# Wide attention of a 16-head layer: the value product with the values stationary, softmax sums by a block of ones, and a new order of the pieces

## The reference, cut to what matters

```
b, s, _ = x.shape
q = (x @ Wq).reshape(b, s, N_HEADS, HEAD_DIM)
k = (x @ Wk).reshape(b, s, N_HEADS, HEAD_DIM)
v = (x @ Wv).reshape(b, s, N_HEADS, HEAD_DIM)
dot = jnp.einsum('bihd,bkhd->bhik', q, k)
w = jax.nn.softmax(dot / jnp.sqrt(jnp.float32(HEAD_DIM)), axis=-1)
a = jnp.einsum('bhij,bjhd->bihd', w, v)
a = a.reshape(b, s, N_HEADS * HEAD_DIM)
return a @ Wo + bo
```

## Time and profile before

| | us |
|---|---|
| median of 3 runs | 2512.74 |
| lowest and highest | 2504.58, 2514.27 |
| the profiled execution | 2513.31 |
| its span, first to last instruction | 2511.3 |
| first matmul of the wide block, to the last DVE instruction of it | 56.9 to 787.3 |

### The profile page before, as it was taken

The page is one execution under the profiler, slowest core; times in us unless marked ns, Lnnn a source line. Parts: engine busy times, 40 slices in busy tenths (PEclk is TensorE's granted clock), DMA queues, the critical chain, the costliest instruction groups (busy, mean ns, idle before and its releaser), DMA issues. The chain is left out here.

```text
span 2511.3 us, 53791 instructions
## 1 busy us (share of the span) xinstructions
PE 2157.5 (86%) x21439; PEld 1560.5 (62%) x21439; DVE 1429.7 (57%) x2854; ACT 1158.7 (46%) x1979; POOL 602.0 (24%) x952
## 2 busy tenths in 40 slices
PE   0899999999998799788868998999669997469996
PEld 0687877877787689655547896666435543234543
DVE  1545454454542443466644445776568885768883
ACT  0333333333324233366553323665647775537774
POOL 4111111111100322133203232443123331433330
PEclk9999999999997899899978998999869998669998
DMA  5000000000000002245400022444134440034441
GB/s 156 1 1 1 1 1 1 1 1 1 1 1 1 6 5 51 51 108 117 95 2 4 1 52 53 109 116 93 25 84 107 110 105 2 2 92 108 107 106 49
DMA packets 142790, 121.04 MB, mean 48 GB/s; under 512 B 11808, under 2 KB 127408, under 8 KB 142548
## 3 DMA queue, kind: packets, MB, share of 16 engines
q1 hardware_dynamic: 142548, 117.64, 19.7%
HBM read 63.48 MB, written 54.12 MB: 47 GB/s over the span
## 5 line engine op out<-in xcount | busy, mean ns | idle before, releaser
L890 DVE TENSOR_REDUCE l_group_mx<-maxima 128x4 f32<-128x1024 f32 x248 | 303.9, 1226 | 77.1 <-PE maxima L683 75.6
L2059 ACT ACTIVATE l_wide_pr<-scores 128x512 f32<-128x512 f32 x256 | 139.0, 594 | 408.7 <-PE scores L2003 408.7
L818 ACT ACTIVATE l_group_pr<-scores 128x1024 f32<-128x1024 f32 x256 | 261.7, 1022 | 72.2 <-PE scores L704 70.0
L2014 PEld LDWEIGHTS bank<-l_wide_va,l_wide_pr 128*128 128x128 f32 x2048 | 254.2, 192 | 36.0 <-issue 33.2
L2014 PE MATMUL bank<-l_wide_va,l_wide_pr 128*128 128x65 f32 x2048 | 254.5, 271 | 0.0
L2098 DVE TENSOR_REDUCE l_wide_mx<-maxima 128x2 f32<-128x512 f32 x256 | 165.1, 687 | 92.2 <-PE maxima L1983 92.2
L2157 POOL CAST l_wide_qk<-l_wide_qk 128x512 bf16<-128x512 f32 x128 | 78.7, 615 | 390.6 <-ACT l_wide_qk L2054 390.6
L890 DVE TENSOR_REDUCE l_slope_mx<-maxima 128x6 f32<-128x768 f32 x124 | 118.9, 959 | 78.2 <-PE maxima L690 76.8
L890 DVE TENSOR_REDUCE l_rope_mx<-maxima 128x6 f32<-128x768 f32 x124 | 118.8, 958 | 58.8 <-PE maxima L690 57.9
L818 ACT ACTIVATE l_slope_pr<-scores 128x768 f32<-128x768 f32 x128 | 103.6, 810 | 91.0 <-PE scores L711 90.8
L724 PE MATMUL bank<-l_group_pr,va 128*32 128x256 f32 x2048 | 145.3, 403 | 0.0
(11 more groups left out here) (456 smaller groups left out, 4721.5 us busy)
## 6 DMA issues: line engine op xcount, KB each, us to landing
l_group_st<-stack_dram SPq DMA_DIRECT2D x64, 384.0 KB, 6.0
l_slope_st<-stack_dram SPq DMA_DIRECT2D x32, 384.0 KB, 5.6
l_rope_st<-stack_dram SPq DMA_DIRECT2D x32, 384.0 KB, 5.6
stack_dram<-l_group_parts SPq DMA_DIRECT2D x64, 192.0 KB, 2.3
stack_dram<-l_group_parts SPq DMA_DIRECT2D x64, 128.0 KB, 1.9
stack_dram<-l_slope_parts SPq DMA_DIRECT2D x32, 192.0 KB, 2.4
stack_dram<-l_rope_parts SPq DMA_DIRECT2D x32, 192.0 KB, 2.3
stack_dram<-l_slope_parts SPq DMA_DIRECT2D x32, 128.0 KB, 2.3
```

Of the source, the lines that this page charges most:

```text
L818: act.activation(pr[:, i % AHEAD, :, 0:keys], Tp[:, :, 0:keys], ACT.Exp).then_inc(s["exps"], 1)
L890: dve.tensor_reduce(mx[:, b % 2, :, :, i], max_bank(i, b)[:, :, 0:BLOCKS * keys].rearrange("p z (a k) -> p z a k", k=keys), AX.X, ALU.max, ...
L2014: ins = pe.matmul(Ob[i // 2 % 2][:, col:col + D64 + 1], pr[:, i % WIDE_AHEAD, kt * S + t * P:kt * S + (t + 1) * P], va[:, par, kt, i, :], ...
L2059: act.activation(pr[:, h % WIDE_AHEAD, :], Tb[h % 2][:], ACT.Exp).then_inc(s["exps"], 1)
```

## The change

The value product is turned round. For a pair of heads the values are stationary, 128 keys by 64 channels, and 256 columns of `pr` (all queries) move; the first head's output lies on PSUM partitions 0 to 63 and the second's on 64 to 127, which puts the two into the left and the right half of PE's columns. The output has channels on partitions, as "project" needs it, so "attn", `att` and the copies to `att_t` are gone. The softmax sums come from a piece of their own, "sum": POOL adds the two key tiles of `pr` into `tiles_sum`, and PE multiplies them by a 128 x 64 block of ones, so the sum stands on the same 64 partitions as the head's values. DVE then takes the reciprocal of all 128 x 256 of them and multiplies. ACT copies the values "v" in place of DVE. "project" is cut into two halves of 128 rows.

The order is new: `wide_slots` has eight slots, one for each pair i, and each holds divide i-2, score i, max i+1, qk i+2, value and sum i-1, and at most one or two of v, xn, norm, project, turnmax, split. `wide_walk` writes out the steps and gives the banks `Mb` in turn. In batch 0 the maxima of odd pairs use the banks `Tb`.

```diff
-WIDE_BANK = {"norm": (0,), "qk": (1, 0, 1, 0, 1, 0, 1, 0), "attn": (1, 0, 1, 0), "v": (1, 0, 1, 0), "project": (1,),
-             "turnmax": (0,)}
-WIDE_AHEAD = 4
...
+def wide_slots():
+    slots = []
+    for i in range(PAIRS):
+        slot = [("divide", (i - 2) % PAIRS, -1 if i < 2 else 0), ("score", i, 0)]
+        slot += [("turnmax", 0, 1)] if i == 7 else []
+        slot += [("max", (i + 1) % PAIRS, 2 if i + 1 >= PAIRS else 1)]
+        slot += [("split", 0, 1)] if i == 6 else []
+        slot += [("qk", (i + 2) % PAIRS, 2 if i + 2 >= PAIRS else 1)]
+        slot += [(what, (i - 1) % PAIRS, -1 if i < 1 else 0) for what in ("value", "sum")]
+        slot += {1: [("v", 0, 1)], 2: [("v", 1, 1)], 3: [("v", 2, 1), ("xn", 0, 2)], 4: [("project", 0, -1)],
+                 5: [("v", 3, 1), ("norm", 0, 2)], 6: [("project", 1, -1)]}.get(i, [])
+        slots += slot
+    return slots
+
+
+def wide_walk():
+
+    slots, order, counts = wide_slots(), [], [0, 0]
+    bank = {}
+    for what, i, _ in slots:
+        if what in ("norm", "qk", "v", "project", "turnmax"):
+            bank[what, i] = len(bank) % 2
+    for n in range(-2, NB + 1):
+        for what, i, ahead in slots:
+            if 0 <= n + ahead < NB:
+                m = bank.get((what, i))
+                if m is not None:
+                    counts[m] += 1
+                order.append((what, i, n + ahead, m, counts[m] if m is not None else None))
+    return order
...
-        va = sb("va", [P, 2, NT, H, D64 + 1])
+        va = sb("va", [P, 2, NT, H, D64])
+        ones = sb("ones", [P, D64])
...
-        pr = sb("pr", [P, WIDE_AHEAD, 2 * S])
-        rc = sb("rc", [P, 4])
-        att = sb("att", [P, 2, NT, H, D64])
-        att_t = sb("att_t", [P, PAIRS, S])
+        pr = sb("pr", [P, 2, 2, 2 * S])
+        tiles_sum = sb("tiles_sum", [P, 2, 2, S])
+        rc = sb("rc", [P, S])
+        att_t = sb("att_t", [P, 2, PAIRS, S])
...
+        def max_banks(i, b):
+            return Tb if b == 0 and i % 2 else Sb
...
-                    elif what == "value":
-                        if i % 2 == 0:
-                            wait(pe, s["divided"], o_t.add() - 2)
-                        pe.wait_ge(s["exps"], exps_t.add())
-                        for t in range(NT):
-                            col = ((i % 2) * NT + t) * (D64 + 1)
-                            for kt in range(NT):
-                                ins = pe.matmul(Ob[i // 2 % 2][:, col:col + D64 + 1],
-                                                pr[:, i % WIDE_AHEAD, kt * S + t * P:kt * S + (t + 1) * P], va[:, par, kt, i, :],
-                                                start=(kt == 0), stop=(kt == NT - 1))
-                        ins.then_inc(s["valued"], 1)
...
-                    elif what == "attn":
-                        if i == 0:
-                            pe.wait_ge(s["divided"], divided_t.add(PAIRS))
-                        for c in range(2):
-                            for t in range(NT):
-                                ins = pe.transpose(bank[:, (c * NT + t) * P:(c * NT + t + 1) * P],
-                                                   att[:, nxt, t, 4 * i + 2 * c:4 * i + 2 * c + 2, :].rearrange("p h d -> p (h d)"),
-                                                   K.ident[:])
-                        ins.then_inc(full[b], 1)
...
+                elif what == "max":
+                    pe.wait_ge(s["half"], p + 1)
+                    wait(pe, s["maxed"], 2 * p - (0 if b else 2))
...
+                elif what == "score":
+                    if i == 0:
+                        copied(pe, "turnmax", 0, b)
+                    wait(pe, s["exps"], 2 * p)
...
+                elif what == "value":
+                    if i == 0:
+                        copied(pe, "v", 3, b)
+                    wait(pe, s["divided"], p - 1)
+                    pe.wait_ge(s["exps"], 2 * p + 2)
+                    for kt in range(NT):
+                        for z in range(2):
+                            ins = pe.matmul(Ob[i % 2][rows(z), 0:S], va[:, at, kt, 2 * i + z, :],
+                                            pr[:, i % 2, z, kt * S:(kt + 1) * S], start=(kt == 0), stop=(kt == NT - 1))
+                    ins.then_inc(s["valued"], 1)
+                elif what == "sum":
+                    pe.wait_ge(s["added"], 2 * p + 2)
+                    for z in range(2):
+                        ins = pe.matmul(Ob[i % 2][rows(z), S:2 * S], ones[:], tiles_sum[:, i % 2, z, :], start=True, stop=True)
+                    ins.then_inc(s["summed"], 1)
+                elif what == "project":
+                    pe.wait_ge(s["divided"], PAIRS * (b + 1))
+                    for c in range(PAIRS):
+                        ins = pe.matmul(bank[:, 0:C], att_t[:, at, c, i * P:(i + 1) * P], W["wo"][:, c, :],
+                                        start=(c == 0), stop=(c == PAIRS - 1))
+                    ins.then_inc(full[m], 1)
...
+                elif what == "v":
+                    act.wait_ge(full[m], count)
+                    act.activation(va[:, at, i // 2, 8 * (i % 2):8 * (i % 2) + 8, :].rearrange("p h d -> p (h d)"),
+                                   Mb[m][:], ACT.Copy).then_inc(drained[m], 1)
+                elif what == "score":
+                    wait(act, s["valued"], p - 1)
+                    wait(act, s["added"], 2 * (p - 1))
+                    for z in range(2):
+                        act.wait_ge(s["scored"], 2 * p + z + 1)
+                        act.activation(pr[:, i % 2, z, :], Tb[z][:], ACT.Exp).then_inc(s["exps"], 1)
...
-                    elif what == "divide":
-                        dve.wait_ge(s["valued"], valued_t.add(2))
-                        o = Ob[i % 2][:, 0:2 * NT * (D64 + 1)].rearrange("p (z t e) -> p t z e", z=2, t=NT)
-                        r = rc[:].rearrange("p (t z) -> p t z", t=NT)
-                        wait(dve, s["divided"], divided_t.value())
-                        own.done(dve.reciprocal(r, o[:, :, :, D64]))
-                        divided_t.add()
-                        dve.tensor_tensor(att[:, par, :, 2 * i:2 * i + 2, :], o[:, :, :, 0:D64],
-                                          r.unsqueeze(3).to_broadcast([P, NT, 2, D64]), ALU.mult).then_inc(s["divided"], 1)
...
+                elif what == "divide":
+                    dve.wait_ge(s["summed"], p + 1)
+                    wait(dve, s["divided"], p)
+                    own.done(dve.reciprocal(rc[:], Ob[i % 2][:, S:2 * S]))
+                    dve.tensor_tensor(att_t[:, at, i, :], Ob[i % 2][:, 0:S], rc[:], ALU.mult).then_inc(s["divided"], 1)
+                elif what == "project":
+                    tile = b * NT + i
+                    dve.wait_ge(s["biased"], b + 1)
+                    dve.wait_ge(full[m], count)
+                    dve.tensor_tensor(K.X[:, tile, :], K.X[:, tile, :], Mb[m][:, 0:C], ALU.add).then_inc(drained[m], 1)
+                    dve.wait_ge(drained[m], count)
+                    dve.bn_stats(K.moments[:, tile, :], K.X[:, tile, :]).then_inc(s["stats"], 1)
...
+                elif what == "score":
+                    wait(pool, s["summed"], p - 1)
+                    for z in range(2):
+                        pool.wait_ge(s["exps"], 2 * p + z + 1)
+                        pool.tensor_tensor(tiles_sum[:, i % 2, z, :], pr[:, i % 2, z, 0:S], pr[:, i % 2, z, S:2 * S],
+                                           ALU.add).then_inc(s["added"], 1)
```

More of the change, by code:

```diff
@@ L1905, in wide_attention @@
 def wide_attention(nc, K, name, W):
-    fills = [sum(b == m for banks in WIDE_BANK.values() for b in banks) for m in range(2)]
     with ExitStack() as ctx:
@@ L1933, in wide_attention @@
         block = ctx.enter_context(nc.Block(name))
-        POOL_SETS = 6
-        def rows(h):
-            return slice(64 * (h % 2), 64 * (h % 2) + 64)
-        def fill_tallies():
-            return [Tally(s["full0"], fills[0]), Tally(s["full1"], fills[1])]
-        def bank_of(tallies, what, i):
-            if what not in WIDE_BANK:
-                return None, None
-            b = WIDE_BANK[what][i]
-            return b, tallies[b].add()
+        POOL_SETS = 7
+        order = wide_walk()
@@ L1948, in _, with rows, copied @@
+        filling = {(what, i, b): (m, count) for what, i, b, m, count in order}
+        def rows(z):
+            return slice(64 * z, 64 * z + 64)
+        def max_banks(i, b):
+            return Tb if b == 0 and i % 2 else Sb
+        def copied(eng, what, i, b):
+            m, count = filling[what, i, b]
+            eng.wait_ge(drained[m], count)
         @block.tensor
         def _(pe):
-            fill = fill_tallies()
-            xn_t, half_t, maxed_t = Tally(s["xn"], 1), Tally(s["half"], PAIRS), Tally(s["maxed"], H)
```

265 lines of the change are left out of this document (88 added, 177 removed).

## The result

| | before | after |
|---|---|---|
| median, us | 2509.22 (4 runs) | 2437.23 (4 runs) |
| lowest and highest | 2504.58, 2514.27 | 2431.62, 2445.55 |
| span of the profiled execution | 2511.3 | 2443.4 |
| last DVE instruction of the wide block ends | 787.3 | 719.6 |
| from there to the end of the span | 1724.0 | 1723.8 |

The ratio is 0.9715, with a 95% interval of 0.9679 to 0.9752: 72 us faster. 2426 was forecast, with 2404 to 2470 as its range, that is a gain of 87 us. The last two rows say where the time came from: the wide block is 67.7 us shorter and the layers behind it take what they took. Between kernels whose later layers are the same instructions that rest varied in the profiles from 1713 to 1726 us, so for edits of the wide block its end is the sharper measure than the time of the launch.

What follows compares the result with a forecast made beforehand. PE was taken as the bound; start 88.0, low clock 3.1, batches 35.0, 504.4, 36.1 and 24.6, tail 9.2 end the wide block at 700.4, not 787.3. 2513.3 less 86.9 gives 2426 us, range 2404 to 2470.

Steps and rivals of the forecast that it cites:

- The bound: Wide block: PE's pieces add up to the batch before and after; DVE, ACT and POOL stay below it.
- Value and sum: PE, per pair: 6 rounds of 0.215 plus 0.14, 1.43 us, in place of 1.86 for two heads' values.
- the quarters of the group layer: Pricing row: value with four heads in quarters of the columns, 16 records in 1.00 us, running four at a time.
- The rival that halves overlap in part: PE's value and sum gain only 1.6 times, 1.75 us a pair, 41 us more: 2467 us; chance 0.10.
- the one that they don't: PE's value and sum in halves never overlap, 2.72 us a pair, 165 us more: 2591 us; chance 0.05.
- The slot and the batch: PE: ordinary slot 3.80 us; eight of them plus v, project, norm and turnmax make 38.8, against 44.53 before.
- DVE: Reciprocal of 128 x 256 at 1.75 us, batch work 29.2; rival with DVE as bound: 2466 us, chance 0.15.
- The margin in slots 7 and 0: About 0.3 us between the end of DVE's maxima and PE's max, after the split and the wait for project.
- ACT and POOL: Work per batch 16.9 and 17.3 us, neither bounding; POOL's adds must not delay the cast for PE's next max.
- The first score: Start of block on PE: at 88 us, each pair waiting 3.0 for qk, copy, cast and max; half-clock rival: 2433.
- The low clock that follows the first score: Wide block after 88.0 us: 3.1 us added, as 7.50 us at clock 0.59 before, assumed to happen again.
- The tail: End of wide block: sum 7 waits for adds, then two divides of 2.25 and both projects in a row, 9.2 us.

Runs made afterwards that it cites:

- Experiment 3: Kernel after, with the reciprocal of only 128 of the 256 columns of sums, used for both halves: 2437.6 us, ratio 0.9724 to the kernel before.
- experiment 6: Kernel after without POOL's adds, PE's sum multiplying both key tiles, four products in place of two: 2497.5 us, ratio 0.9946 to the kernel before.
- experiment 5: Kernel after with each head's value product on all 128 columns, outputs of the two heads mixed: 2551.9 us, ratio 1.018 to the kernel before.
- experiment 1: Kernel after with v, norm, xn and project moved between qk and value of their slot: 2419.7 us, ratio 0.9653 to the kernel before.
- experiment 4: Kernel after with each reciprocal done twice: 2505.7 us, ratio 0.9985 to the kernel before.
- experiment 2: Kernel after with qk i+2 ahead of max i+1 in the steps before the first scores: 2432.9 us, ratio 0.972 to the kernel before.
- experiment 8: Kernel after with v, norm, xn, project between qk and value, and qk ahead of max before the first scores: 2415.2 us, ratio 0.963 to the kernel before.

## Why the prediction was right, and what it mis-sized

*The bound.* PE alone, before and after: right. Experiment 3 shows it for DVE, where half of the new work changed no batch, and experiment 6 for POOL, where taking the adds away gave nothing back.

*Value and sum.* 1.43 us a pair was forecast from the quarters of the group layer, 1.44 was measured. The rival that halves overlap in part is out (0.91 against 1.82 in experiment 5), so is the one that they don't: two halves gained 2.0. Had they not overlapped the kernel would have been slower, by 1.8% for the values alone (2551.9); the rival's 2591 counts the sums too.

*The slot and the batch.* 3.80 was forecast and 3.91 measured, 38.8 and 40.0. This is the step that was too small. I had priced qk, v and project from rows in which a piece on the full array followed them. The 0.11 of "handover" that I added to a qk's 0.86 is the price of coming back to the full array from a max; the 0.09 of leaving it was missing. In the new order it falls on the eight qk, which stand ahead of a value in halves, 0.7 us a batch, on three of the four v, 0.3 (the fourth stands ahead of norm and costs the old 0.97), and on the halves of project, 0.2. Experiment 5 shows it the other way: with the value on the full array, qk costs 0.97 again. The Trainium skill, "TensorEngine Tiling (Array Packing)", section "Key Properties", says that changing the tiling mode drains the TensorE. The trace agrees in that a change costs time (0.2 us for a v's stretch, experiment 1); of a drain itself it shows only that the next weight load doesn't start ahead. I had left the rule out of the sum because the number of changes a pair seemed to fall.

*DVE.* The reciprocal was forecast at 1.75 us from three rows of 4 to 32 columns; it is 1.753. (The sum as written, 353 + 224 x 6.2, gives 1.742.) The Trainium skill's repeat count of 8 ("VectorE: DVE Perf Modes", the 8-slice pipeline), from which 2.3 us were estimated, doesn't fit if it is read as eight cycles a column: 954 ns for 128 columns and 1753 for 256 are 6.24 ns a column. DVE's busy time a batch was forecast at 29.2 and is 30.2; the reciprocals are not the cause, 8 x 1.753 being the 14.0 of the sum, and where the 1.0 lies was not traced. The margin in slots 7 and 0 was forecast at 0.3 us and is 1.0 (the maxima end at 405.70, PE's max starts at 406.72), in part since I counted gaps where the records overlap (experiment 4).

*ACT and POOL.* 16.9 and 17.3 a batch forecast, 16.8 and 16.5 measured; the adds are hidden (experiment 6).

*The ends.* The first score was forecast at 88 and came at 89.8. I had the chain at full clock, 3.0 us a pair, and one us for a slow start; it ran at 4.08 for three pairs, 3.86 for one and 2.92 from there. The low clock that follows the first score in the earlier trace rows didn't come back (fast records and 1.00 from 90 us on), 3.1 less. That was luck: experiments 3 and 4 have the same instructions up to the first score, and their clock fell there, to 0.68 and 0.63 from 88 to 91 us, though it cost them less than 3.1, some 1.3 us in experiment 3. The tail was forecast at 9.2 and took 11.1, 1.6 of it by the low clock in project. The errors sum up: 1.8 for the start, 15.0 for the batches (18 less the 3.1), 0.5 and 1.9 for the last batch and the tail, 19.2 in all, which is 719.6 against 700.4. The launch came out only 11 us above the forecast, because the profiled execution was the slowest of the four, 8 us above their median, while the forecast was summed from a profiled execution close to its median: that too is luck, and the gain that was forecast, 87 us, was 15 too large.

## What to carry to other kernels

On PE, count the stretches on the full array in the written order as well as the columns: pieces that use the whole array belong side by side, and putting them so was worth 17 us here with the same instructions. When a piece is priced from a row, look at what stands ahead of it and behind it there, and whether both will be of the same shape in the new place. Turning a product round so that its narrow side fills half of the array paid here only since two such products run beside each other (without it the kernel is 1.8% slower) and since the sums are made cheap elsewhere: POOL's hidden adds were 55 of the 72 us, and without them the turned product was no better than the old one in the same order. Price an instruction of a new size from a line through several sizes of the same operation; it gave the reciprocal within 1%.

## What the runs showed of the hardware that was not expected

- A reciprocal on DVE costs 6.24 ns a column (954 ns at 128, 1753 at 256), so 256 columns take four times what a multiply of that shape takes (424 ns). An operation that was negligible at four columns became DVE's largest.
- A qk of four records costs 0.86 us between pieces on the full array, 0.97 behind a max and ahead of a piece on the full array, and 1.06 behind a max and ahead of a value in halves; at a change of shape the next weight load starts with its product and not 0.2 us ahead of it (experiment 1).
- DVE's instructions follow each other with starts up to 0.08 us before the end of the last record; a chain of them is shorter than the sum of their durations.
- PE's records were slow by a factor of two at the start while it alternated 2.6 us of products with 1.5 us of waiting, and with two qk back to back they became fast some 10 us earlier. The profile's granted clock, 1.00 throughout that stretch, doesn't show it.
- The clock fell or stayed behind the same wait: after 3.2 us without products ahead of the last project it was 0.70 in the kernel after and 1.00 in experiments 1, 2 and 8.
